# GpSimd's edge loop cut into a long loop of sixteen visits a turn and a short loop of two

## Time and profile before

| what | value |
|---|---|
| median of three runs | 2377.72 us |
| the profiled execution's own time | 2377.29 us |
| its span, first to last instruction | 2375.5 us |
| TensorE busy | 2208.2 us (93%) |
| VectorE busy | 2132.9 us (90%) |
| ScalarE busy | 1927.9 us (81%) |
| GpSimd busy | 1641.4 us (69%) |

### The profile page before, as it was taken

How to read it: one execution, slowest core, us unless ns; L and a number is a source line. 1 busy time by engine, 2 the same in 40 slices (tenths; PEclk the granted TensorE clock), 3 DMA queues, 4 the chain that set the end, 5 groups by cost and what they waited for, 6 DMA issues and landing times. The chain is left out here.

```text
span 2375.5 us, 50565 instructions
## 1 busy us (share of the span) xinstructions
PE 2208.2 (93%) x12061; PEld 1809.9 (76%) x12061; DVE 2132.9 (90%) x6133; ACT 1927.9 (81%) x4051; POOL 1641.4 (69%) x1693
## 2 busy tenths in 40 slices
PE   7499799999999999999999999999999999999988
PEld 6255588887888888887888888878888888878867
DVE  6587699999999999999999999999999999999967
ACT  3477588888888888888888888888888888888857
POOL 1671477777777777777777777777777777777730
PEclk9699899999999999999999999999999999999999
DMA  7698799999999999999999999999999999999964
GB/s 281 164 242 284 244 283 282 279 282 272 281 280 280 284 281 285 279 280 274 282 282 281 284 281 280 282 273 284 278 280 283 283 280 282 278 279 279 282 203 146
DMA packets 300661, 642.52 MB, mean 270 GB/s; under 512 B 63260, under 2 KB 120976, under 8 KB 300632
## 3 DMA queue, kind: packets, MB, share of 16 engines
q0 software_dynamic: 129840, 418.70, 60.0%
q1 hardware_dynamic: 168888, 217.10, 30.5%
q10 hardware_dynamic: 1904, 6.40, 0.7%
HBM read 583.36 MB, written 58.64 MB: 270 GB/s over the span
## 5 line engine op out<-in xcount | busy, mean ns | idle before, releaser
L954 POOL DMA_INDIRECT e_kv<-kv_tab,e_idx x1568 | 1532.5, 977 | 489.7 <-issue 442.1
L1083 ACT ACTIVATE e_gate_ps<-e_gate_ps 128x1024 f32<-128x1024 f32 x786 | 765.6, 1002 | 247.7 <-PE e_gate_ps L1015 247.6
L1155 DVE TENSOR_TENSOR e_gated<-e_kv,e_gate_ps 128x1024 f32<-128x1024 f32 x788 | 932.0, 1210 | 26.7 <-issue 19.5
L1002 PE MATMUL e_sum_ps<-e_gated,weighed_hot 128*128 128x256 f32 x3168 | 749.1, 379 | 2.1 <-ACT weighed_hot L1099 2.1
L1014 PE MATMUL e_gate_ps<-wd_hi_lo,high 128*128 128x512 f32 x1572 | 639.3, 407 | 92.7 <-DVE e_gated L1155 92.1
L1002 PEld LDWEIGHTS e_sum_ps<-e_gated,weighed_hot 128*128 128x128 f32 x3168 | 600.1, 190 | 98.5 <-ACT weighed_hot L1099 2.7
L1015 PE MATMUL e_gate_ps<-wd_bias,low 128*128 128x512 f32 x1572 | 620.2, 395 | 0.0
L1164 DVE CUSTOM_DVE_ANT_0 e_gated<-e_gated,e_q_ps 128x256 f32<-128x256 f32 x1576 | 571.4, 409 | 1.0 <-PE e_q_ps L1034 1.0
L1099 ACT ACTIVATE weighed_hot<-hot,e_attn 128x128 f32<-128x128 bf16 x1580 | 520.1, 401 | 41.1 <-DVE e_attn L1174 32.9
L1014 PEld LDWEIGHTS e_gate_ps<-wd_hi_lo,high 128*128 128x128 f32 x1572 | 296.2, 188 | 224.0 <-issue 90.4
L1033 PE MATMUL e_q_ps<-q_win,hot_t 128*128 128x256 f32 x1572 | 424.0, 303 | 0.6 <-DVE e_dot L1164 0.6
(11 more groups left out here) (159 smaller groups left out, 1332.6 us busy)
## 6 DMA issues: line engine op xcount, KB each, us to landing
e_attr<-attr_groups_dram SPq DMA_DIRECT2D x784, 128.0 KB
e_q_next<-q_tab SPq DMA_DIRECT2D x98, 256.0 KB
e_kv<-kv_tab,e_idx POOLq DMA_INDIRECT x1568
sum_tab<-e_sums SPq DMA_DIRECT2D x100, 128.0 KB
e_prior<-sum_tab SPq DMA_DIRECT2D x99, 128.0 KB
kv_tab<-l_kv_out SPq DMA_DIRECT2D x49, 256.0 KB, 4.8
q_tab<-l_q_out SPq DMA_DIRECT2D x49, 256.0 KB, 3.7
sum_tab<-zeros SPq DMA_DIRECT2D x25, 256.0 KB, 2.8
```

The costliest lines, as they stand in the source:

```text
L954: pool.indirect_dma_start(kv[:, k, :], None, kv_tab, bass.IndirectOffsetOnAxis(ap=idx[:, at:at + 1], axis=0)).then_inc(kv_landed[k // G][k ...
L1002: last = nc.tensor.matmul(sum_ps[:, 0:H], weighed_hot[:, c % 2, k, :], gated[:, c * G + k, H:2 * H], start=(c == 0 and k == 0), stop=(c == ...
L1083: nc.scalar.activation(gate_ps[:, 2 * p:2 * p + 2, :], gate_ps[:, 2 * p:2 * p + 2, :], ACT.Silu).then_inc(silu_ready[s][p], 1)
L1155: nc.vector.tensor_tensor(gated[:, pair(s, p), :], kv[:, pair(s, p), :], gate_ps[:, 2 * p:2 * p + 2, :], ALU.mult).then_inc(gated_ready[s] ...
```

## The change

GpSimd's loop is written as two loops one behind the other. The first has a body of eight pairs of visits (sixteen visits), the second the old body of one pair. Two new values, worked out by three more VectorE instructions behind L374, give their turns: `long_turns = (pairs - 1) >> 3` and `short_turns = pairs - 8 * long_turns`. For 49 pairs that is six long turns (96 visits) and one short turn (2 visits). Gathers, waits, registers and their order stay as they are. The instruction of L374 now also goes through `then`. The other engines' loops are not touched.

```diff
-                    nc.vector.tensor_single_scalar(pairs_of_visits[:], pairs_of_visits[:], 1, ALU.arith_shift_right)
+                    then(nc.vector.tensor_single_scalar(pairs_of_visits[:], pairs_of_visits[:], 1, ALU.arith_shift_right))
+
+                    then(nc.vector.tensor_scalar(long_turns[:], pairs_of_visits[:], -1.0, None, ALU.add))
+                    then(nc.vector.tensor_single_scalar(long_turns[:], long_turns[:], 3, ALU.arith_shift_right))
+                    nc.vector.scalar_tensor_tensor(out=short_turns[:], in0=long_turns[:], scalar=-8.0, in1=pairs_of_visits[:], op0=ALU.mult, op1=ALU.add)
...
-                with pool.Fori(0, pool.value_load(pairs_of_visits[0:1, 0:1], min_val=(BLOCKS + 1) // 2, max_val=(BLOCKS * -(-N // P) + 1) // 2)):
+                fewest, most = (BLOCKS + 1) // 2, (BLOCKS * -(-N // P) + 1) // 2
+                assert fewest > 8
+                with pool.Fori(0, pool.value_load(long_turns[0:1, 0:1], min_val=(fewest - 1) // 8, max_val=(most - 1) // 8)):
+                    for i in range(8):
+                        gather_visit(0)
+                        gather_visit(1)
+                with pool.Fori(0, pool.value_load(short_turns[0:1, 0:1], min_val=1, max_val=8)):
                     gather_visit(0)
                     gather_visit(1)
```

More of the change, by code:

```diff
@@ L96, in gnn_kernel @@
         pairs_of_visits = keep("pairs_of_visits", [P, 1], I32)
+        long_turns = keep("long_turns", [P, 1], I32)
+        short_turns = keep("short_turns", [P, 1], I32)
         zeros = keep("zeros", [P, 2 * H], F32)
@@ L389, in gnn_kernel @@
         edge_stage(nc, dict(
-            ident_bf=ident_bf, iota=iota, steps=steps, src_tiles=src_tiles, dst_f=dst_f, cut=cut, window_f=window_f, walk=walk, total=total, pairs_of_visits=pairs_of_visits,
+            ident_bf=ident_bf, iota=iota, steps=steps, src_tiles=src_tiles, dst_f=dst_f, cut=cut, window_f=window_f, walk=walk, total=total, long_turns=long_turns, short_turns=short_turns,
             wd_hi_lo=wd_hi_lo, wd_bias=wd_bias, q_tab=q_tab, kv_tab=kv_tab, sum_tab=sum_tab, attr_groups=attr_groups,
@@ L806, in edge_stage @@
 def edge_stage(nc, shared):
-    ident_bf, iota, steps, src_tiles, dst_f, cut, window_f, walk, total, pairs_of_visits, wd_hi_lo, wd_bias = (
-        shared[n] for n in ("ident_bf", "iota", "steps", "src_tiles", "dst_f", "cut", "window_f", "walk", "total", "pairs_of_visits", "wd_hi_lo", "wd_bias"))
+    ident_bf, iota, steps, src_tiles, dst_f, cut, window_f, walk, total, long_turns, short_turns, wd_hi_lo, wd_bias = (
+        shared[n] for n in ("ident_bf", "iota", "steps", "src_tiles", "dst_f", "cut", "window_f", "walk", "total", "long_turns", "short_turns", "wd_hi_lo", "wd_bias"))
     q_tab, kv_tab, sum_tab, attr_groups, NP, N, BLOCKS = (
```

## The result

The changed kernel takes 2387.45 us (median of 5 runs, 2385.73 to 2390.46), the one before 2377.72. The ratio is 1.0045, with a 95% interval of 1.0034 to 1.0056: slower by 9.7 us. The profiled execution has a span of 2385.5 us, against 2375.5 before.

What follows compares the result with a forecast made beforehand. TensorE and VectorE, waiting for one another, were taken to set the 20.6 us visit. Four slips at 1.2 us plus one at 3.8 made 8.6 us; added to 2377.3 this gave 2385.9 us, range 2376 to 2397.

Steps and rivals of the forecast that it cites:

- Mechanism: GpSimd's long loop: each of five branches back fetches the body's start anew, delaying the next visit's gathers; 8.6 us lost.
- The signs: About 25 instruction packets between 300 and 2300 us; idle about 1.6 us ahead of four gathers, about 4 ahead of 512.
- Turns and the small additions: GpSimd's 42 removed branches gain 0; three VectorE instructions, one more wait and a second register load cost 0.
- A body of 545 doesn't stay loaded: GpSimd's long body of 545 instructions, against 69 before, outgrows what stays loaded, so five branches back each need a fetch.
- The price of a fetch: Sequencer's wait behind a branch back: 4.2 us, mean wait for a landing in the edge stage; bounds 1.8 and 7.1.
- Cover and slips: At GpSimd's branches back, 2.9 us of sequencer lead hides part of a fetch; gathers slip 1.3 us four times, 3.8 at 512.
- What a slip costs: Edge stage loses 1.2 us for each slip of 1.3 and 3.8 for the one of 3.8; 8.6 us together.
- hidden fetch: Rival: at GpSimd's branches back the fetch takes 3.2 us or less, or none happens; 2377 to 2380 us, chance 0.36.
- turns cost today: Rival: GpSimd starts late at each turn of the old loop, so 42 turns save 12 us; 2365 us, chance 0.07.
- every block of code stalls: Rival: about 4 code blocks a turn each stall inside GpSimd's body, 29 us, 2406 us; chance 0.10 together with 7 us stalls.

Runs made afterwards that it cites:

- one long turn: The changed kernel with 48 pairs (96 visits) in the long body, so the long loop never branches back; 2376.33 us, ratio 1.0002 to the kernel before.
- the hint for the way back: The changed kernel with the long loop written as nc.Fori with hint_back_edge=True, naming the body's start ahead of the branch; 2380.17 us, ratio 1.0012.

## Why the prediction was right, point by point

- **Mechanism.** The start of the long body is fetched anew at five branches, GpSimd's sequencer waits, and VectorE pays at L1167. Shown: packets on q14, the sequencer's five halts, and the loss gone without a branch back and with a body of 273 instructions. The signs came but for two: some 25 packets were forecast and 34 came, and two of the five gaps stayed at 0.30 us. Forecast 2385.9 us, measured 2387.45; forecast loss 8.6, measured 9.7, of which 7.9 in the loop. That the sum came so close is in part luck: two slips forecast at 1.3 were 0, two were 1.9, the one at gather 512 was 4.4 in place of 3.8, and these nearly cancel.
- **Turns and the small additions cost and bring nothing.** Shown by one long turn and by four visits a turn.
- **A body of 545 doesn't stay loaded.** Right: 34 packets came in during the loop. Ahead of the result this was my estimate; the longest body seen to stay loaded was TensorE's of about 224. On GpSimd one of 273 stayed and one of 341 already didn't. Code that came in straight on cost nothing: 25 packets in the one long turn, no loss.
- **The price of a fetch, 4.2 us from a store's landing.** Measured 3.2, 3.3 and three times 4.7, mean 4.1. That a store's landing comes so close is luck: no run ties the two.
- **Cover and slips.** Mis-sized for the single turn. 4 x 1.3 and 3.8 were predicted, 0, 4.4, 1.9, 0 and 1.9 measured: 9.0 and 8.2 in sum. The cover is 2.9 at a usual turn, but at gathers 256 and 1024 the gather came 4.7 us behind the branch, so 3.5 us of cover met the two short fetches. The equal slip at four turns was an average that no turn has. The late sequencer ahead of gather 512 came again, as assumed: 4.7 us of halt less 0.4 of cover are the 4.4 within 0.1.
- **What a slip costs.** Predicted 8.6 us for all five, measured 7.6 in VectorE's waits and 7.9 in the loop, for 8.2 us of slips. That is about one us for a us of slip in the sum, but not a price of each slip. The prediction counted four gaps in the trace before; there are nine of this kind, of 0.84 to 1.38 us (the last section lists them), and VectorE's seven waits stand behind four of them. The other five cost it nothing. With fourteen visits a turn 5.8 us of slips came with 7.9 us more of waits.
- **The rivals.** The hidden fetch is what two of five turns show. That turns cost today, and that every block of code stalls, both fell with the one long turn. The four blocks a turn in the prediction stood in no row; the one long turn brought 25 packets in 96 visits, 4.2 for each sixteen.

Open: why three fetches took 4.7 us and two 3.2 to 3.3. In the trace the fetch's packet starts 2.0 and 2.1 us behind the branch at the two short ones and 3.1 to 3.2 at the three long ones, and the sequencer goes on 1.6 to 1.9 us after that at all five; so most of the difference is time before the packet starts. With ten, twelve and fourteen visits a turn the halts take any length from 3.0 to 5.0 us. The two short ones fell where GpSimd was running late, at another place between the other transfers; I did not test whether that is the cause. Open too is why VectorE pays more for some slips than for others.

## What to carry to other kernels

Before unrolling an engine's loop, look whether its turn leaves the engine idle at all: here the idle time ahead of a gather was 0.30 us with a turn or without, so there was nothing to win. Count the body's recorded instructions, and look for packets of kind instruction inside the loop: where the body stayed loaded there were none, or one or two in the whole loop, and a body that outgrew that paid for its branches back, as far as the cover didn't hide them. What a halt of the sequencer cost was set here by how far it ran ahead; a wait that holds it close to its engine (here the one that AHEAD sets) can be worth more than the loop's form.

## What the runs showed of the hardware that was not expected

- A body of 273 recorded instructions stayed loaded on GpSimd, one of 341 did not; code came in packets of 8 KB, an estimated 131 instructions each. Where between 273 and 341 the limit lies was not measured.
- With the hint for the way back the way out came late: 6.9 us from the branch that isn't taken to the next gather, with 3.05 us idle, where the changed kernel without the hint has 4.1 and 0.30.
- The gaps of the earlier trace rows are gathers 211 and 1411; others of their kind in the same trace are 112, 311, 611, 711, 1011, 1111 and 1511. They lie hundreds of gathers apart, and every run with AHEAD = 10 has such gaps, whatever the loop. The sequencer stands still there for 3.4 us, where it usually takes about 1.0 for a gather. With AHEAD = 12 it still does, but no gather is late. What halts the sequencer there was not found. With the halts hidden VectorE's waits for gathered rows fall by 3.7 us; the kernel before became 5.0 us faster with 12, and the rest of that was not traced.
